# Cross attention with 16 heads over 8192 keys: key and value projection and attention in one pass

## What is computed

```python
def _L0_xattn_ref(query, key, value, cached_key, cached_value, ...):
    E, H, D = (512, 16, 32)
    q = (jnp.einsum('bqe,fe->bqf', query, wq) + bq).reshape(B, Lq, H, D)
    k = (jnp.einsum('bke,fe->bkf', k_full, wk) + bk).reshape(B, Lkv, H, D)
    v = (jnp.einsum('bke,fe->bkf', v_full, wv) + bv).reshape(B, Lkv, H, D)
    scores = jnp.einsum('bqhd,bkhd->bhqk', q, k) * scale
    attn = jax.nn.softmax(scores, axis=-1)
    ctx = jnp.einsum('bhqk,bkhd->bqhd', attn, v).reshape(B, Lq, E)
    out = jnp.einsum('bqe,fe->bqf', ctx, out_proj_weight) + out_proj_bias
x = x + _L0_xattn_ref(_layernorm(x), ctx_1024, ctx_1024, ctx_1024, ctx_1024, ...)
x = x + _L0_attn_ref(_layernorm(x), ...)
x = x + _L0_ffn_ref(_layernorm(x), ...)
```

## Time and profile before

| | |
|---|---|
| Median of 3 runs (lowest, highest) | 1454.82 us (1450.03, 1454.9) |
| Profiled execution: its own time, its span | 1445.7 us, 1443.9 us |
| TensorE matmuls busy | 1370.8 us (95%), 7608 instructions |
| VectorE busy | 950.6 us (66%) |
| ScalarE busy | 772.9 us (54%) |
| GpSimd busy | 73.6 us (5%) |
| Mean granted TensorE clock | 0.964 |
| DMA moved | 225.07 MB, of it 162.61 MB read from HBM and 59.85 MB written |

### The profile page before, as it was taken

The page is one execution under the profiler, slowest core; times in us unless marked ns, Lnnn a source line. Parts: engine busy times, 40 slices in busy tenths (PEclk is TensorE's granted clock), DMA queues, the critical chain, the costliest instruction groups (busy, mean ns, idle before and its releaser), DMA issues. The chain is left out here.

```text
span 1443.9 us, 20528 instructions
## 1 busy us (share of the span) xinstructions
PE 1370.8 (95%) x7608; PEld 847.3 (59%) x7608; DVE 950.6 (66%) x819; ACT 772.9 (54%) x841; POOL 73.6 (5%) x71
## 2 busy tenths in 40 slices
PE   5999999999799999999999999998769999999995
PEld 4888888888643333333333333333557787887873
DVE  7444444444288888888888888887653566766662
ACT  4122221221088888888888888884222445555541
POOL 2000000000030000000000000000102010111110
PEclk9999999999999999999999999999955999999998
DMA  6854555556396555555555555520804666676641
GB/s 207 266 175 179 193 199 184 174 193 196 136 260 131 112 112 112 112 109 114 116 116 116 116 116 116 114 61 1 306 5 147 220 216 211 232 243 206 239 132 40
DMA packets 140900, 225.07 MB, mean 156 GB/s; under 512 B 8776, under 2 KB 41672, under 8 KB 140848
## 3 DMA queue, kind: packets, MB, share of 16 engines
q1 hardware_dynamic: 137520, 217.12, 51.7%
q0 software_dynamic: 3344, 7.47, 2.1%
HBM read 162.61 MB, written 59.85 MB: 154 GB/s over the span
## 5 line engine op out<-in xcount | busy, mean ns | idle before, releaser
L663 ACT ACTIVATE at_p<-at_s 128x1024 f32<-128x1024 f32 x512 | 496.9, 1023 | 90.7 <-PE at_s L616 90.6
L683 DVE TENSOR_TENSOR p_sum<-p_sum,at_p 128x2048 f32 (+1 forms) x208 | 476.7, 2292 | 58.1 <-ACT at_p L663 51.1
L616 PEld LDWEIGHTS at_s<-q_stack,at_k 97*128 97x128 f32 x1024 | 172.7, 189 | 248.5 <-ACT at_p L663 162.0
L616 PE MATMUL at_s<-q_stack,at_k 97*128 (+1 forms) x1024 | 311.4, 424 | 7.5 <-PEq L444 6.7
L629 PE MATMUL at_o<-at_p,at_v 128*32 128x512 f32 x2048 | 272.7, 605 | 0.1
L143 ACT ACTIVATE sc_c_hi<-sc_c 128x2048 fp32r<-128x2048 f32 x16 | 30.7, 1920 | 151.0 <-PE sc_vp L388 137.6
L413 ACT ACTIVATE sc_k_hi<-sc_kp,sc_bk 128x512 fp32r<-128x512 f32 x64 | 44.2, 691 | 125.4 <-PE sc_kp L381 125.4
L345 DVE SCALAR_TENSOR_TENSOR sc_k_lo<-sc_kp,sc_bk,sc_k_hi 128x512 fp32r<-128x512 f32 x64 | 47.8, 749 | 89.0 <-ACT sc_k_hi L413 89.0
L353 DVE TENSOR_TENSOR sc_v<-sc_vp,sc_bv 128x512 f32<-128x512 f32 x64 | 44.1, 689 | 88.8 <-PE sc_vp L388 88.8
L1268 ACT ACTIVATE se_h<-se_hp,se_b_cur 128x160 f32<-128x160 f32 x128 | 43.4, 391 | 105.4 <-PE se_hp L1203 105.4
L1255 ACT ACTIVATE se_wi_hi<-ei_wi 128x2048 fp32r<-128x2048 f32 x32 | 61.2, 1913 | 69.4 <-DVE se_b_cur L1314 69.1
(11 more groups left out here) (225 smaller groups left out, 1534.4 us busy)
## 6 DMA issues: line engine op xcount, KB each, us to landing
at_k<-k_hi_scratch SPq DMA_DIRECT2D x128, 256.0 KB, 4.8
ei_wi<-w_in SPq DMA_DIRECT2D x32, 1024.0 KB, 7.4
ei_wo<-w_out SPq DMA_DIRECT2D x32, 1024.0 KB, 5.5
sc_c<-ctx_t SPq DMA_DIRECT2D x16, 1024.0 KB, 7.9
k_hi_scratch<-sc_k_hi SPq DMA_DIRECT2D x16, 1024.0 KB, 4.0
k_lo_scratch<-sc_k_lo SPq DMA_DIRECT2D x16, 1024.0 KB, 6.1
at_k<-k_lo_scratch SPq DMA_DIRECT2D x64, 256.0 KB, 4.2
at_v<-v_scratch SPq DMA_DIRECT2D x64, 256.0 KB, 4.9
```

Source lines behind the costliest of these rows:

```text
L616: last = nc.tensor.matmul(s[r][:, a * NQ:(a + 1) * NQ], k[c][:, j, t * P:(t + 1) * P], q_stack[:, bass.ds(it // PER_GROUP * (HG * NQ) + j ...
L663: nc.scalar.activation(p[t % PR][:, pair * 2 * NQ:(pair + 1) * 2 * NQ], s[u % SR][:, :], ACT.Exp, scale=SCALE).then_inc(p_ready[t % PR], 1)
L683: nc.vector.tensor_tensor(sums, sums, p[t % PR][:, :], ALU.add).then_inc(p_summed[t % PR], 1)
```

## The change

`stream_context`, the scratch tensors in HBM, `find_maxima` and `attend` are replaced on the normal path by one block, `attend_stream`. For a chunk of 512 keys it goes through 16 steps (4 head groups by 4 key tiles), two of them to a double j, and projects the keys and values of the next chunk between them, one product of 12 matmuls in a double, through one PSUM bank. Keys and values stay in SBUF. The first chunk is projected before the loop, in eight banks.

The scores of a tile are now twelve matmuls with 32 rows: three parts (hi by hi, lo by hi, hi by lo) of four heads, each head in its own 32 rows of the array and its own bank. The weights are read where the projection left them, so nothing is stacked.

VectorE adds all tiles to `p_sum`; `BY_PE` and `total_acc` are gone. It adds the output bank to `o_acc` once per chunk and head group, ahead of the next tile's sum. The values' bias is left out of `v` and enters at the end of `cross_output` through the output weights, in four more matmuls.

The flag for the general path comes from the logarithms of the sums and is read once, at the end: a last block holds the whole layer again (`any_path`, the old code) under one condition on each engine. `route` puts both conditions (an expert too long, a sum too large or small) in one number. These inputs leave it out, as before. The last output DMA is now waited for before that block (`sp.wait_ge(r.stored, 16)`), not in it.

In `send_to_experts` the four turned tiles of the tokens come first and the four of the tail behind them. The values' bias comes in four small DMAs.

```diff
-    BY_PE = (4, 9, 15)
...
-                for a in range(2):
-                    j = 2 * pair + a
-                    last = nc.tensor.matmul(s[r][:, a * NQ:(a + 1) * NQ], k[c][:, j, t * P:(t + 1) * P],
-                                            q_stack[:, bass.ds(it // PER_GROUP * (HG * NQ) + j * NQ, NQ)],
-                                            start=True, stop=True)
...
+def attend_stream(nc, ctx, c_dram, o_acc, p_sum, a, late, late_dram):
+    SR, PR = 3, 4
+    STEPS = NG * KT
+    DOUBLES = STEPS // 2
+    OUTPUTS = [("v", 0), ("k", 0), ("v", 1), ("k", 1), ("v", 2), ("k", 2), ("v", 3), ("k", 3)]
...
+            def scores(i, b, step):
+                n, g, t = 2 * i + b, step // KT, step % KT
+                if t == 0:
+                    pe.wait_ge(k_lo_ready, NG * n + g + 1)
...
+                for part, (keys, queries) in enumerate(((k_hi, q_hi), (k_lo, q_hi), (k_hi, q_lo))):
+                    for j in range(HG):
+                        rows, r = slice(j * D, (j + 1) * D), ((b * STEPS + step) * 2 + j // 2) % SR
+                        last = nc.tensor.matmul(s[r][:, j % 2 * NQ:(j % 2 + 1) * NQ], keys[rows, g, t * P:(t + 1) * P],
+                                                queries[rows, g, :], start=(part == 0), stop=(part == 2))
+                        if part == 2 and j % 2 == 1:
+                            last.then_inc(s_ready[r], 1)
...
+            def pair(i, last):
+                for b in range(2):
+                    n = 2 * i + b
+                    begins, ends = isinstance(n, int) and n == 0, last and b == 1
+                    for j in range(DOUBLES):
+                        scores(i, b, 2 * j)
+                        if j == 0 and not begins:
+                            project(n, b, *OUTPUTS[-1], proj[:, :], False)
+                        elif j > 0 and not ends:
+                            project(n + 1, 1 - b, *OUTPUTS[j - 1], proj[:, :], False)
+                        scores(i, b, 2 * j + 1)
+                        for step in (2 * j - 2, 2 * j - 1):
+                            if step >= 0:
+                                outputs(n, b, step)
+                            elif not begins:
+                                outputs(n - 1, 1 - b, step + STEPS)
...
+                    for j in range(DOUBLES):
+                        exps(i, b, 2 * j)
+                        if j == 0 and not begins:
+                            keep(n, b, *OUTPUTS[-1], proj[:, :])
+                        elif j > 0 and not ends:
+                            keep(n + 1, 1 - b, *OUTPUTS[j - 1], proj[:, :])
+                        if 2 <= j < 2 + ET and not last:
+                            split(n + 2, b, j - 2)
+                        exps(i, b, 2 * j + 1)
...
+                    for j in range(DOUBLES):
+                        if j % 2 == 1 and j > 1:
+                            add_outputs(n, (j - 3) // 2)
+                        elif j == 1 and not begins:
+                            add_outputs(n - 1, NG - 1)
+                        add_probabilities(n, 2 * j)
+                        if j == 0 and not begins:
+                            keep_low(n, OUTPUTS[-1][1], proj[:, :])
+                        elif j > 0 and not ends and OUTPUTS[j - 1][0] == "k":
+                            keep_low(n + 1, OUTPUTS[j - 1][1], proj[:, :])
+                        if 2 <= j < 2 + ET and not last:
+                            split(n + 2, b, j - 2)
+                        add_probabilities(n, 2 * j + 1)
...
+            pe.wait_ge(widened, NG + 1)
+            for g in range(NG):
+                last = nc.tensor.matmul(out[0][:, :], bv_wide[:, g, :], wo[:, g, :], start=(g == 0), stop=(g == NG - 1))
+            last.then_inc(bias_done, 1)
+            pe.wait_ge(bias_added, 1)
...
+                nc.vector.tensor_reduce(widest[:, :], log[:, :, :].rearrange("p g q -> p (g q)"), X, ALU.max,
+                                        apply_absolute_value=True).then_inc(topped, 1)
...
+            sp.wait_ge(r.stored, 16)
...
                 for d in range(ET):
                     nc.tensor.transpose(turn[:, d, 0:P], tokens[:, d * P:(d + 1) * P], ident[:, :])
+                for d in range(ET):
                     last = nc.tensor.transpose(turn[:, d, P:CAP], tail_tokens[:, d * P:(d + 1) * P], ident[0:D, 0:D])
                 last.then_inc(turned, 1)
```

More of the change, by code:

```diff
@@ L911, in route @@
         "ro_weights_turned", "ro_combine_t_ready", "ro_ranked", "ro_hi_ready", "ro_done"))
-    with nc.Block() as block:
+    with opened() as block:
         @block.sync
@@ new lines, in run_stages, with meet, run, _ @@
+def run_stages(nc, stages, again, met):
+    def meet(eng, times):
+        eng.drain()
+        eng.sem_inc(met, 1)
+        eng.wait_ge(met, 5 * times)
+    def run(eng, name):
+        flag = eng.value_load(again[:, :], min_val=0, max_val=1)
+        with eng.If(flag > 0):
+            for k, stage in enumerate(stages):
+                if name == "gpsimd":
+                    for first in (n for n in stage.retired if n - 1 not in stage.retired):
+                        end = next(n for n in range(first, first + len(stage.retired) + 1) if n not in stage.retired)
+                        nc.gpsimd.sem_clear(range(first, end))
+                meet(eng, 2 * k + 1)
+                if name in stage.programs:
+                    stage.programs[name](eng)
+                meet(eng, 2 * k + 2)
+    with nc.Block() as block:
+        @block.sync
+        def _(sp):
+            run(sp, "sync")
+        @block.gpsimd
+        def _(pool):
+            run(pool, "gpsimd")
+        @block.vector
+        def _(dve):
+            run(dve, "vector")
+        @block.tensor
+        def _(pe):
+            run(pe, "tensor")
+        @block.scalar
+        def _(act):
+            run(act, "scalar")
```

1281 lines of the change are left out of this document (719 added, 562 removed).

## The result

The changed kernel takes **1398.17 us** (median of 4 runs, 1394.64 to 1399.35), the one before 1453.07 us (4 runs, 1450.03 to 1454.9): ratio 0.9637, 95% interval 0.9615 to 0.9659. The profiled execution took 1399.07 us, its span is 1397.3 us. The forecast was 1343 us: it was right in sign, the time lies inside the range, but half of the gain is missing. 110 us were forecast and 55 came.

What follows compares the result with a forecast made beforehand. TensorE was taken to set the pace; 1445.7 - 105.4 (stream and attention) - 4 (turned tokens) + 1.5 (end) = 1337.8 us, forecast as a 1343 us median. Own range 1310 to 1365 us, with B 1310 to 1420 us.

Steps and rivals of the forecast that it cites:

- Scores: Attention's score matmuls: row groups overlap like column groups, 0.89 us a tile, 227.8 us for 256 tiles.
- A: Scores: weight loads into different row groups queue, 1.69 us a tile, +205 us, 1548 us; chance 0.12.
- C: Scores: no overlap at all, 2.99 us a tile, 1881 us; chance 0.03 together with rival D.
- B: Fused stage: score rounds of 0.3 us, or ScalarE and VectorE late at times; 1370 to 1420 us; chance 0.27.
- change of form: TensorE switching the array's form: 0.19 us in a tile's scores, from draining and an uncovered first weight load.
- Projection, outputs, the double: Fused stage on TensorE: 2.99 us per projection product, 1.86 us for two tiles' outputs, 6.63 us a double.
- VectorE's and ScalarE's room: Work in a 6.63 us double: VectorE at most 5.9 us, ScalarE 5.1 us, so both fit.
- Turned tokens: Experts' token transposes: grouping the forms saves 0.6 us, seven times, -4 us (bounds 0 and -9).
- Start and end: Bias loads at the start cost 0; the last block's branch after the output lands costs +1.5 us (0 to 4).
- Cross output: Behind the attention: four new float32 matmuls and the new maximum are covered by other work, taken as 0.
- Rival D: Whole layer: general path taken behind the fast one, over 2700 us; chance 0.03 together with C.
- 5 us for entering and leaving: Ends of the fused stage: last keys of the first chunk, splits of chunk 1 and last outputs, 5 us.

Runs made afterwards that it cites:

- hinted loop: The changed kernel with a hint naming the back edge at the top of each pass of TensorE's loop: 1364.02 us.
- entry and end mended: Hinted loop plus chunk 1's splits and exponential's table moved earlier, last chunk's outputs between score steps, bank's addition ahead of the second sum: 1357.06 us.
- passes of two: The kernel before, with two iterations in each pass of TensorE's attention loop: 1450.06 us, ratio 1.0004.
- passes of four: The kernel before, with four iterations in each pass of TensorE's attention loop: 1457.17 us, ratio 1.0043.

## Why the prediction was right and where it was wrong

*Scores, the term that was said to decide*: right, 0.92 and 0.90 us for 0.89. Rivals A and C fall with it, and so does the row-group part of B. No run shows the rounds of 0.3 us that B's range was built with: the second round starts 0.34 us after the first and the third 0.23 us after the second (400.31, 400.65 and 400.88 us), and the first two of the full matmuls that follow are as far apart as the first two rounds (0.34 us, then 0.23). All four heads on one row group take 2.94 us a step, 3.2 times 0.92. A load of 32x128 takes 184 ns on the mean, and four are over in 0.19 us, so their number cost nothing. What the 0.19 us for a change of form are made of, which the prediction calls draining and a first load, no run takes apart; that they are there shows (0.11 us more behind the first round, as much behind the last).

*Projection, outputs, the double*: right, 2.99, 1.86 and 6.65 us. *VectorE's and ScalarE's room*: right inside a double; that depends on the order of VectorE's queue, as the 92 us of the bank's addition show. The busy shares were forecast too high (85% and 75%; 695 and 606 of 909.6 us are 76% and 67%).

*Turned tokens*: -4 us forecast; 0.51 us seven times is -3.6 us, and the run in the old order shows that it is the order (40.06 us an expert again). *Start and end*: from TensorE's last matmuls to the end of the span it is 17.45 us (1379.85 to 1397.3) against 15.5 before, 1.9 us more for 1.5 forecast. *Cross output*: from its first column sum to the first matmul of the self attention 33.3 us for 32.6, so 0.8 us where nothing was forecast. *Self attention and routing*: no term in the forecast; 3.0 us more, with the lower clock. *Rival D*: the general path was not run.

*The step that failed*: **the sum was made of equal doubles, each at the price of TensorE's own work, with 5 us for entering and leaving, and nothing for the loop**. The stage took 909.6 us up to the cross output's first sum, 56 us more than the forecast's saving allows (49 us came of 105). Where they went:

- 34 us: five taken back edges, 25 us of stops and the lower clock behind them. The prediction named no term for it at all. The loops of its trace jump back without a stop (216 matmuls in a pass of the attention, no gap over 0.5 us). One jump in it takes longer: the 6.3 us of the earlier trace rows hold the jump over the block that is left out, whose record lasts 3.35 us. The prediction took that gap as a price for the end of the kernel and not for the loop, although the change makes a pass of TensorE about four times as long (216 to 832 matmuls).
- 10 us: the last chunk. Seven doubles without a projection were priced as TensorE's work alone (3.64 us); they took 5.1 us, because the projection had hidden the time through ScalarE.
- 7 us: the entry. The first eight products took 24.1 us instead of 22.4 (the clock was at 0.68 in their first 5 us), TensorE waited 1.83 us before them, and the first two doubles took 17.3 us for 8.4 us of work, 8.9 us more (waits of 4.38 and 1.20 us for ScalarE, and the clock at 0.70); 5 of all this were in the forecast.
- 4 us: 6.65 instead of 6.63 us a double, and 0.3 us at each border of a pair.

- 1 us: TensorE waits 1.97 us for the ones of the column sums, 1.21 before.

The five make 56; each is rounded.

Rival B had the right region (1370 to 1420 us), and the stated range holds the measured time only by B's part of it. That is luck: its mechanisms were not what happened, neither rounds of 0.3 us nor engines late in every double. ScalarE was late only at the entry and in the last chunk (between 75 and 890 us TensorE waits for it once, 0.2 us). A hinted loop gives 1364 us, and with entry and end mended 1357 us, which leaves 14 us to the forecast: the last chunk at 4.5 instead of 3.64 us, clock losses at the start, and the borders.

What I had not weighed is what a jump back costs when a pass is long. In the trace the jump's record lasts 3.3 to 3.8 us at the five stops, with packets of the instruction queue beside it, and 0.25 us at most with the hint. A pass with 832 matmuls and 832 weight loads (1738 records in all) stops without the hint and not with it; a pass with 432 and 432 jumps back with no packet fetched. No length between the two was tried.

## What to carry to other kernels

When a change makes a loop's pass much longer, count the instructions of each engine in a pass and look at its back edges: the gap on one engine with "issue" as its cause (4.7 to 5.4 us, some 113.5 us apart), behind which all others ran dry, was a jump back here; writing the pairs out and hinting the edge both removed it (1364.82 and 1364.02 us for 1398.17), and a longer pass only made it rarer (two stops for five). Price the first and the last pass by themselves: what the middle of a pipeline hides can be bare at its ends, as the 5.1 us of a double in the last chunk for 3.64 us of TensorE's work. And in a queue of mixed work the small item that another engine waits for goes first: an addition of 0.7 us behind a sum of 2.3 us cost 92 us.

## What the runs showed of the hardware

- A taken back edge of TensorE stopped it for 4.7 to 5.4 us with 832 matmuls and as many loads in a pass, for 2.0 us in the kernel before with 864, and not visibly with 432 or 216. The jump's own record lasts 3.3 to 3.8 us in both kernels where it stops, and 0.21 to 0.26 us where it does not or is hinted; the matmuls issued ahead of the jump go on for 1.8 us behind its record's start in both kernels (271.18 to 272.98 us, 657.60 to 659.37 us), so the stop seen is shorter by that. ScalarE's and VectorE's back edges in the same stage showed no cost (1396.99 us with both written out, 1398.17 us with their loops).
- Packets of the instruction queue over the whole execution: 22 in the kernel before, 24 with passes of two, 49 with passes of four (two stops), 31 with these hinted; 75 in the changed kernel (five stops), 31 hinted, 64 with TensorE's pairs written out (more code, no stop). So for the same code in a loop a stop goes together with fetching: 44 and 18 packets more, about nine of 16 KB for each jump back.
- Matmuls on the four row groups of 32 rows overlapped fully here: four start within 3 to 23 ns, the second round 0.34 us after the first and the third 0.23 us after it, the distances of single full matmuls in the same double. They also passed each other: with three parts of one head in a row the trace still has rounds of four heads, and a double is only some 0.03 us longer (6.68 us for 6.65).
- With all scores on one row group TensorE was busy for 95% of the span, and its mean clock was 0.863 (0.951 in the changed kernel), with doubles of 10.73 us at the upper level and mostly 12.3 to 13.9 us where a part of them ran at the lower one (a clock of 0.74 from 743 to 757 us). What makes it fall there was not tried.
